# Second expert weights and their bias laid out once as one row per partition, in a fused patch-embedding, attention and expert kernel

## The reference

```python
def body(acc, p):
    w1, bb1, w2, bb2, g = p
    h = jax.nn.gelu(xn2 @ w1 + bb1, approximate=False)
    return (acc + g[:, None] * (h @ w2 + bb2), None)
moe_out, _ = jax.lax.scan(body, jnp.zeros_like(xn2), (W1, b1, W2, b2, gates_full.T))
return x + moe_out.reshape(Bx, Nx, C)
```

## Time and profile before

| what | value |
|---|---|
| median of 3 runs | 2596.96 us (2594.35 to 2597.08) |
| profiled execution | 2601.49 us |
| its span | 2599.6 us |
| TensorE busy | 2382.5 us (92%) |
| VectorE busy | 1658.9 us (64%) |
| ScalarE busy | 1158.6 us (45%) |
| GpSimd busy | 1042.2 us (40%) |
| mean of the DMA traffic | 101 GB/s |

### The profile page before, as it was taken

One profiled execution on the slowest core, in us unless ns is written; L12 is line 12 of the kernel. 1 busy time (PEld: TensorE's weight loads), 2 busy tenths in 40 slices (PEclk: granted clock), 3 DMA queues, 4 the chain that ended last, 5 costly groups with the idle time before them and its releaser, 6 DMA issues. The chain is left out here.

```text
span 2599.6 us, 64053 instructions
## 1 busy us (share of the span) xinstructions
PE 2382.5 (92%) x19496; PEld 1836.3 (71%) x19496; DVE 1658.9 (64%) x4146; ACT 1158.6 (45%) x2240; POOL 1042.2 (40%) x1196
## 2 busy tenths in 40 slices
PE   5589999999999999999999999999999988999886
PEld 4456666666666666677777777777777667888886
DVE  3558888888888888867767776777667731111111
ACT  2234443444433444355555565555555643333332
POOL 2103333333333333244444444444444454555555
PEclk8679999999999998899999999999999999999998
DMA  7432222321223222544344455544534356878774
GB/s 136 150 40 33 33 34 46 45 32 33 34 41 50 32 32 36 135 91 97 102 110 98 106 114 118 113 96 106 117 89 104 95 158 197 219 209 226 203 214 122
DMA packets 250837, 262.98 MB, mean 101 GB/s; under 512 B 35477, under 2 KB 230489, under 8 KB 250777
## 3 DMA queue, kind: packets, MB, share of 16 engines
q1 hardware_dynamic: 213912, 229.95, 37.2%
q0 software_dynamic: 36864, 32.27, 7.2%
HBM read 212.21 MB, written 52.83 MB: 102 GB/s over the span
## 5 line engine op out<-in xcount | busy, mean ns | idle before, releaser
L1347 DVE TENSOR_REDUCE MX<-PS 108x2 f32<-108x648 f32 x576 | 456.0, 824 | 45.6 <-PE PS L1769 40.9
L1042 ACT ACTIVATE pool<-PS 108x648 f32<-108x648 f32 x576 | 387.4, 714 | 216.5 <-PE PS L1792 186.4
L890 POOL DMA_INDIRECT out<-big,tokn x192 | 304.2, 1584 | 436.2 <-DVE big L1497 232.2
L1648 PE MATMUL PS<-WB,big 128*128 128x192 f32 x2304 | 406.3, 332 | 2.5 <-ACT big L1071 2.5
L1071 ACT ACTIVATE big<-PS,WF 128x256 f32<-128x256 f32 x576 | 242.2, 473 | 371.6 <-PE PS L1648 369.9
L1648 PE MATMUL PS<-XE,WF 128*128 128x256 f16 x2880 | 366.4, 279 | 35.3 <-DMA WF<-w1p 28.2
L1648 PEld LDWEIGHTS PS<-WB,big 128*128 128x128 f32 x2304 | 375.6, 192 | 27.4 <-issue 18.5
L1648 PEld LDWEIGHTS PS<-XE,WF 128*128 128x128 f16 x2880 | 277.9, 100 | 91.2 <-issue 33.5
L867 POOL DMA_INDIRECT xbuf<-XR,DST x192 | 190.5, 992 | 242.5 <-issue 197.8
L1497 DVE SCALAR_TENSOR_TENSOR big<-PS,grow,GB 128x192 f32<-128x192 f32 x192 | 71.3, 413 | 273.5 <-POOL GB L878 144.2
L1803 PE MATMUL PS<-pool,Vp 108*32 108x324 f32 x2304 | 217.5, 520 | 0.0
(11 more groups left out here) (197 smaller groups left out, 4104.1 us busy)
## 6 DMA issues: line engine op xcount, KB each, us to landing
WF<-w1p SPq DMA_DIRECT2D x96, 771.5 KB, 5.1
WB<-in_L_ffn_W SPq DMA_DIRECT2D x96, 576.0 KB, 4.7
ximg<-in_x SPq DMA_DIRECT2D x96, 196.0 KB, 5.3
XtR<-xbuf SPq DMA_DIRECT2D x96, 196.0 KB, 2.5
ximg<-in_x SPq DMA_DIRECT2D x96, 195.1 KB, 8.7
B2t<-in_L_ffn_b SPq DMA_DIRECT2D x96, 96.0 KB, 5.3
out<-R SPq DMA_DIRECT2D x32, 243.0 KB
w1p<-WF SPq DMA_DIRECT2D x8, 768.0 KB, 4.0
```

What stands on the lines that cost most here:

```text
L890: nc.gpsimd.indirect_dma_start(rows_out, bass.IndirectOffsetOnAxis(ap=tokn[:, i, s_:s_ + 1], axis=0), Yt[:, i, s_, :], None, bounds_check= ...
L1042: nc.scalar.activation(Pr[:, at:at + 2, :], pair(("st", p))[0:TP, :, 0:T], ACT.Exp, scale=SCALE2).then_inc(S["ex"], 1)
L1347: nc.vector.tensor_reduce(MX[:, qt, g, 64 * jj:64 * jj + 64:32], pair(("s", p))[0:TP, :, 0:T], AX.X, ALU.max).then_inc(S["mx"], 1)
L1648: last = nc.tensor.matmul(out_ap, lhsT, rhs, start=(i == 0), stop=(i == len(products) - 1))
```

## The change

A second copy of the expert weights, `w2p` (8 x 128 x 1344 numbers), is made in memory once: its row for a partition holds the six pieces of `w2` and then `b2`. It is written by nine transfers from memory to memory, one for all biases (1024 rows of 768 bytes) after the second turn, and one for each expert (768 rows of 768 bytes) after the third. They are waited for in SP's stream ahead of the turn in which the first tiles are loaded. A tile's load then is one transfer of 128 rows of 5376 bytes; B2t becomes a view of the end of WB2, and the down semaphores count 16 a tile.

```diff
+W2ROW = NC * D + D
...
-        WB2 = sb("WB2", [128, 3, NC, D], F32)
-        attS = WB2[:, 0, :, :]
...
-        B2t = sb("B2t", [128, 3, D], F32)
+        WB2 = sb("WB2", [128, 3, W2ROW], F32)
+        attS = WB2[:, 0, 0:NC * D].rearrange("p (c d) -> p c d", c=NC)
...
+        B2t = WB2[:, :, NC * D:]
...
-                sp.dma_start(WB2[:, i, :, :], w2[bass.ds(e, 1), :, :].rearrange("a (c p) n -> p (a c) n", p=128)
+                sp.dma_start(WB2[:, i, :], w2p[bass.ds(e, 1), :, :].rearrange("a p n -> (a p) n")
                              ).then_inc(S[f"down{i}"], 16)
-                sp.dma_start(B2t[:, i, :], b2[bass.ds(e, 1), :].to_broadcast([128, D])).then_inc(S[f"down{i}"], 16)
...
             sp.dma_start(w1p[:, :, 2 * HID:].rearrange("e p n -> p e n"), b1s[:, :, :]).then_inc(b1_out, 16)
-            with sp.Fori(2, LAG - 1) as b:
+            sp.dma_start(w2p[:, :, NC * D:].rearrange("e p n -> p e n"),
+                         b2.rearrange("(a e) n -> a e n", a=1).to_broadcast([128, E, D])).then_inc(b2_out, 16)
+            run(Turn(ATTEND, 2, 1, 0, None))
+            for e in range(E):
+                sp.dma_start(w2p[e, :, 0:NC * D].rearrange("p (c n) -> p c n", c=NC), w2[e].rearrange("(c p) n -> p c n", p=128)
+                             ).then_inc(w2_out, 16)
+            with sp.Fori(3, LAG - 1) as b:
                 run(Turn(ATTEND, Batch(b), Batch(b) - 1, Batch(b) - 2, None))
             sp.wait_ge(b1_out, 16)
+            sp.wait_ge(b2_out, 16)
+            sp.wait_ge(w2_out, 16 * E)
...
-                pool.wait_ge(S[f"down{i}"], due(f"down{i}", m, 32))
+                pool.wait_ge(S[f"down{i}"], due(f"down{i}", m, 16))
...
-                    pe.wait_ge(S[f"down{i}"], due(f"down{i}", m, 32))
+                    pe.wait_ge(S[f"down{i}"], due(f"down{i}", m, 16))
```

More of the change, by code:

```diff
@@ L76 @@
 EXPERT = dict(
-    rows0=16, rows1=16, rows2=16, up0=16, up1=16, up2=16, down0=32, down1=32, down2=32, gm=PER_TURN, gs=PER_TURN, gb=PER_TURN, ad0=32, ad1=32, ad2=32,
+    rows0=16, rows1=16, rows2=16, up0=16, up1=16, up2=16, down0=16, down1=16, down2=16, gm=PER_TURN, gs=PER_TURN, gb=PER_TURN, ad0=32, ad1=32, ad2=32,
     x_full=PER_TURN, w1=3 * PER_TURN, o_full=PER_TURN, x_evac=PER_TURN, gelu=3 * PER_TURN, y_done=PER_TURN)
@@ L343, in build_program @@
 def build_program(nc, x, txt, tok_w, tok_b, wq, wk, wv, n1w, n1b, qkv_w, qkv_b, proj_w, proj_b, n2w, n2b,
-                  w_gate, w1, b1, w2, b2, const, xbuf, w1p, qbd, out):
+                  w_gate, w1, b1, w2, b2, const, xbuf, w1p, w2p, qbd, out):
     with ExitStack() as ctx:
@@ L429, in build_program @@
         WB1 = WF1[:, :, 0:2 * HID].bitcast(F16)
-        WB2 = sb("WB2", [128, 3, NC, D], F32)
-        attS = WB2[:, 0, :, :]
-        slot = [WB2[:, 1:3, :, :].rearrange("p r c d -> p (r c d)")[:, HID * i:HID * (i + 1)] for i in range(3)]
-        B2t = sb("B2t", [128, 3, D], F32)
+        WB2 = sb("WB2", [128, 3, W2ROW], F32)
+        attS = WB2[:, 0, 0:NC * D].rearrange("p (c d) -> p c d", c=NC)
+        slot = [WB2[:, 1:3, :].rearrange("p r n -> p (r n)")[:, HID * i:HID * (i + 1)] for i in range(3)]
+        B2t = WB2[:, :, NC * D:]
         XtR = sb("XtR", [128, 3, 2, XROW], F32)
@@ L468, in build_program @@
         att_hi, att_lo, stg_hi, stg_lo = sem("att_hi"), sem("att_lo"), sem("stg_hi"), sem("stg_lo")
+        w2_out, b2_out = sem("w2_out"), sem("b2_out")
         pad_set, tok_dup = sem("pad_set"), sem("tok_dup")
@@ L1461, in tables @@
                         dve.wait_ge(S[f"up{i}"], due(f"up{i}", GR * g - 1, 16))
-                        dve.wait_ge(S[f"down{i}"], due(f"down{i}", GR * g - 1, 32))
+                        dve.wait_ge(S[f"down{i}"], due(f"down{i}", GR * g - 1, 16))
                     dve.wait_ge(pad_out, 16 * (E * g + 1))
@@ L1861, in w2_half @@
                     pe.wait_ge(S["gelu"], due("gelu", m, 3 * i + 3))
-                    pe.wait_ge(S[f"down{i}"], due(f"down{i}", m, 32))
+                    pe.wait_ge(S[f"down{i}"], due(f"down{i}", m, 16))
                     free(pe, turn, ("W2", i, 0))
                 last = chain(bank(("W2", i, 0))[:, D * s_:D * s_ + D],
-                             [(hid[:, i, c, 128 * s_:128 * s_ + 128], WB2[:, i, c, :]) for c in range(NC)])
+                             [(hid[:, i, c, 128 * s_:128 * s_ + 128], WB2[:, i, D * c:D * c + D]) for c in range(NC)])
                 if s_ == 1:
@@ L2022 @@
     w1p = nc.dram_tensor("w1p", (E, 128, W1ROW), F32, kind="Internal").ap()
+    w2p = nc.dram_tensor("w2p", (E, 128, W2ROW), F32, kind="Internal").ap()
     qbd = nc.dram_tensor("qbd", (3 * D,), F32, kind="Internal").ap()
-    build_program(nc, *args, xbuf, w1p, qbd, out)
+    build_program(nc, *args, xbuf, w1p, w2p, qbd, out)
     return run(nc, [arrays], core_ids=[0]).results[0]["out"]
```

## The result

The changed kernel takes 2574.85 us (median of 4 runs, 2573.1 to 2576.85) against 2595.65 for the kernel before (median of 4 runs, 2589.12 to 2597.08). The ratio is 0.9925, 95% interval 0.9906 to 0.9944: 0.75% faster, outside the 0.2% that a measurement can tell. The forecast had the sign, but said 2591, and its range ended at 2578, 3 us above the result.

The account below looks back on a forecast made before the run. The last stage was taken as a chain of adds slowed by loads, with TensorE close behind. Terms -10 (tile loads), -1 (switch) and +5 (copies) gave -6 us, 2591 us on the median's scale, range 2578 to 2615 for 8 in 10.

Parts of the forecast that it names:

- The tile loads in the last stage: Last stage, tiles alone: merging the WB and B2t loads saves 0.23 us a step, 10 us over 43 steps.
- the 12.6 that the landings gave: Last stage: whole-run landing times make the merged load 29% shorter, 0.29 us a step, 12.6 us over 43 steps.
- The 2.45 us: Last stage: the part of each 8.75 us add step put down to loads running beside the adds.
- The lower end, nothing: Last stage: no gain from the tile loads, since full engines moved 312 and 307 GB/s behind WB and WF.
- The upper end of 21 us: Last stage: gain from the tile loads if B2t's landing of 7.0 us in that stage alone is used.
- what is late next: Last stage: once the loads are shorter, TensorE itself is late next; its 32 us of idle time leave room.
- One issue fewer on SP: SP's queue: removing the 96 B2t issues brings nothing by itself; 0.6 us a tile if SP were behind.
- The switch: Switch to the second group's tiles: VectorE's wait for the pair shortens, worth 0 to 1.3 us, taken as 1 us.
- The copies: SP's queue after the second turn's `keep`: eight weight copies make batch 3's text late, costing 5 us; bias copy hidden.
- The rival in which reading and writing take turns: Weight copies run at half pace, 49.6 us; batch 3's text is 30 us late, 2616 us in all; chance 0.13.
- Nothing in the last stage: Rival: 768-byte rows already have the full rate, so the tile loads gain nothing; 2596 to 2601 us; chance 0.30.
- Long rows hold the adds up: Rival, last stage: adds wait behind long rows, 1.3 us a turn, 19 us and no gain; 2620 us; chance 0.15.

Follow-up runs that it names:

- copies-only kernel: The kernel before with the nine copies and their waits added and its loads unchanged; ratio 0.9997 (0.9982 to 1.0012).

## Why the prediction was wrong

**The tile loads in the last stage: the place was right, the size was not.** The term was 0.23 us a step and 10 us, between 0 and 21. Measured: 0.55 us a step and 23.7 us, or 0.45 us and 19.4 against the copies-only kernel, about twice the forecast either way. This is the term that was mis-sized. Four things stand in its place.

*The clock had no term.* Of the 23.7 us, TensorE's idle time is 12.9 us. That this is near the 12.6 that the landings gave is chance, as the source of the bias, below, is in it. The rest, 10.8 us, is TensorE's own work getting faster. The kernel before, behind the wait for a first weight that ended at 2300.20:

```profile
2300.20 2.31 PE L1648 MATMUL PS<-XE,WF 128*128 128x256 f16 x10 [3.60 <-DMA WF<-w1p]
```

```profile
2299.80:2303.20 3.40, 3.00 (x18) 2.33 (x19) 0.46 (x3) 0.58 (x2) 0.28 (x1) 0.51 0.94 332
2303.20:2351.00 47.80, 44.56 (x349) 41.62 (x348) 6.73 (x27) 18.28 (x41) 27.69 (x24) 1.00 0.79 210
2351.00:2354.40 3.40, 3.40 (x22) 2.62 (x20) 0.45 (x3) 1.54 (x3) 0.81 (x1) 0.51 0.93 310
```

TensorE waited 3.60 us, and at the end of the wait the granted clock was 0.51 for 3.4 us, that is the lower of its two levels (1.2 instead of 2.4 GHz); the same 47.8 us later. The changed kernel has a stretch of 215 us without such a fall:

```profile
2318.50:2533.50 215.00, 202.43 (x1603) 190.38 (x1600) 31.81 (x132) 83.06 (x187) 123.89 (x107) 1.00 0.79 225
```

The kernel before has seven such stretches in its 43 steps, of 3.4 us and one of 6.8, together 25.4 us inside them; the changed kernel has two, together 5.9 us. Ten matmuls of the first weights take 2.31 us at the lower level and 1.26 at the higher, so about half of such a stretch is lost: 12.7 us before and 3.0 after, which makes 9.7 of the 10.8 us. The others fit roughly: kernels with 0.97 are busy for 342 to 344 us in the 43 steps, those with 0.98 for 334 to 342, those with 0.99 for 333 to 336, with 2607 to 2658 matmuls on record.

What brings the clock down is not shown. Each of the nine stretches begins within some 1.3 us of the end of a wait of TensorE, of 2.06 to 3.94 us. But in the same profile two waits of that size brought none, since the matmuls behind them are at full speed:

```profile
2273.88 1.26 PE L1648 MATMUL PS<-XE,WF 128*128 128x256 f16 x10 [3.00 <-DMA WF<-w1p]
...
2427.93 1.26 PE L1648 MATMUL PS<-XE,WF 128*128 128x256 f16 x10 [2.75 <-DMA WF<-w1p]
```

and the stretch of 215 us without a fall has waits of up to 1.93 us. No experiment takes a wait away and nothing else. The prediction said that TensorE's idle time left room for the gain; it gave no price to what the clock loses around the waits.

*The source of the bias had no term either.* The sum priced rows by length and number. The kernel with the bias from different rows shows 0.26 us a step at equal length and number; the kernel with long weight rows and one bias row shows 0.21 us the other way round. The landings of the adds say the same. From 2190 to 2540 us they are, for the kernel before, the changed kernel, the one with short rows in one transfer and the one without a bias load:

```profile
out<-big,tokn POOLq DMA_INDIRECT x81, 5.4
...
out<-big,tokn POOLq DMA_INDIRECT x86, 4.6
...
out<-big,tokn POOLq DMA_INDIRECT x85, 4.5
...
out<-big,tokn POOLq DMA_INDIRECT x84, 4.4
```

The copies-only kernel has 5.5, and the changed kernel's second profile 4.1. So adds land sooner where the 128 reads of the one row are gone, whatever the length of the weights' rows.

*The 2.45 us were not all the loads'.* I put the difference between 8.75 us and the 6.30 us of the last steps down to the loads, and 41% of it, 1.0 us, to WB and B2t. But TensorE alone is busy for 333.17 / 43 = 7.75 us a step in the changed kernel, so a step could never have come near 6.30. With the 576 KB of weights gone and the bias from its new source the step is 8.07 us, 0.58 to 0.68 less than before (8.65 or 8.75). So the 1.0 us was too much, and the 29% of it that the change was to save too little, and the two errors partly made up for each other.

*One of my ends was read wrongly.* The lower end, nothing, rested on equal rates in two short windows, one of which had adds in it (21.0% of the DMA engines' time from 2297 to 2300.5, 0.2% from 2301 to 2306). Over the whole stretch the traffic rose from 215 to 230 GB/s at the same share. The upper end of 21 us, from the landings of the last stage alone, was the better number, but by luck in part: it has the clock and the source of the bias in it without naming them.

Against the step of the copies-only kernel the gains add up within the spread: different bias rows give 0.26 us (8.65 to 8.39), long weight rows 0.21 (8.65 to 8.44), both together 0.45 (to 8.20). Leaving the weights out altogether gives 0.13 more. TensorE is near, as "what is late next" said.

**One issue fewer on SP:** counted as nothing, and the kernel with two transfers shows that it is nothing.

**The switch:** 1 us forecast, 1.06 measured up to the table. Behind it TensorE's wait for the first rows went from 10.15 to 9.71 us only, within the 0 to 1.3 of the forecast.

**The copies:** 5 us forecast, 1 us in the profile and nothing in the runs of the copies alone. The step that failed was the pace: 4608 KB went in some 17 us, from 218 to about 235, which is some 270 KB/us, faster than even WF's 221. The pace was taken from issue to landing of a single load, with a fixed part taken off. Here the engines were full (share 1.02) with many transfers behind one another. The rival in which reading and writing take turns is refuted by the same row, and so is its price of 30 us.

**The rivals.** "Nothing in the last stage" is refuted, and with it what the 512-byte figure of the Trainium skill ("DMA: Bandwidth & Descriptors", Specifications) would have made of this change: with the bias load the same, rows longer than 768 bytes still took 0.12 us off a step (8.32 to 8.20, one transfer), 0.17 (8.39 to 8.22, two) and 0.21 (8.65 to 8.44, one bias row), three times the same sign. Each is near the spread of 0.1 us by itself, and the second and the third pair are each from two chips; in times the first pair is clear (2582.34 against 2575.66 us on one chip) and the third too (0.9997 against 0.9937), the second is not (0.9946 against 0.9935). From 384 to 768 bytes it was 0.27. "Long rows hold the adds up" is refuted: with the same bias source adds land in 4.6 us beside long rows and in 4.5 beside short ones, and every kernel with long rows has a shorter step than its twin with short ones. Whether an engine's turns between queues go by such packets no run here shows; the price that I feared from it did not come. The rows of the new load went whole: the profile counts 182825 - 150249 = 32576 packets of 2 to 8 KB instead of 20288, which is 12288 or 96 x 128 more.

**What the profile was to show:** the middle stage within 2 us, right (from the 18th to the 31st stored result 937.8 us instead of 936.1). GpSimd's wait for its adds down by 10 us: 19. The step 8.5 us: 8.20. WB landing in 4.5 to 5 us: 6.6, wrong, and 5.4 in the second profile of the same kernel. In the last stage two of these loads out of three are issued one right behind the other. The time to landing of one load says little of what it costs the engines. The table's wait 4.7 us: 4.95. An idle gap of 5 us before VectorE's statistics in turn 3: none.

## What to carry to other kernels

Where one engine is nearly always busy and its few waits come from transfers, ask what the granted clock does around those waits: here 13 us less waiting came with 11 us of faster work, 10 of which are the clock's. A load that repeats one row of memory for all partitions should be priced by itself, not by its bytes; laying it out once, beside an earlier stage, cost nothing that could be measured here (0.9997). Before more work goes into a load, leave it out once and look: without the weights a step of the last stage would have been only 0.13 us shorter. And take the busy time of the nearest engine as the floor of a step, not the shortest step that the trace shows.

## What the runs showed of the hardware that I had not expected

- Transfers from memory to memory in 768-byte rows ran at 301 GB/s on the 16 engines, at a share of 1.02, and SP was held for 10.88 us by eight issues that otherwise take 0.3 to 0.4 us each.
- Reading one 768-byte row 128 times cost more than reading 128 rows of the copy: 0.26 us a tile in the step of the adds (8.39 against 8.65 us). The adds landed in 5.4 and 5.5 us beside it and in 4.1 to 4.6 where it was gone. By which mechanism was not tried.
- TensorE's clock was at its lower level for 3.4 us from the end of a wait of 3.60 us on, and behind waits of 2.06 and 2.49 us too, but not behind one of 3.00 us. A stage whose waits were fewer kept 0.99 instead of 0.97.
